# Retention phase: keys transposed by DMA, and the queries' product ahead of the state updates

## The chip, the cores and the metric

The kernel runs on one core of one Trainium2 chip. The metric is device time in microseconds (us); lower is better. The core's engines are TensorE (PE; its weight loads are listed as PEld), VectorE (DVE), ScalarE (ACT), GpSimd (POOL) and SyncE (SP, which here only issues DMA transfers). Each runs its own instructions in order and waits for others on semaphores.

## The reference

Two layers over 4 x 2048 tokens of 256 features. Each layer adds `s * silu(g)` to its input, where `s` is an attention and `g` a feed-forward network on the layer-normalised input. The change touches only the attention of the second layer, a retention:

```python
x = x + s * g
xn = _layernorm(x, axis=-1)
s = _L1_attn_ref(xn, L1_attn_W_q, L1_attn_W_k, L1_attn_W_v, L1_attn_W_o, L1_attn_gn_weight, L1_attn_gn_bias)
...
# inside _L1_attn_ref, 16 heads of 16 features
gammas = 1.0 - 2.0 ** (-5.0 - jnp.arange(h, dtype=jnp.float32))
q = (x @ W_q.T).reshape(b, t, h, dh)
k = (x @ W_k.T).reshape(b, t, h, dh)
v = (x @ W_v.T).reshape(b, t, h, dh)
decay = jnp.where(diff >= 0, gammas[:, None, None] ** pow_, 0.0)
attn = jnp.einsum('bihd,bjhd->bhij', q, k) * decay[None] / scale
y = jnp.einsum('bhij,bjhd->bihd', attn, v)
```

`y` is then normalised over tokens and heads and multiplied by `W_o`.

## The kernel before

The program is a row of phases, each with a block of instructions per engine and a barrier behind it. The phase in question is `phase_retention` (L1993 on). It goes over the 64 tiles of 128 tokens in a chunked form: a tile is cut into two sub-blocks of 64 tokens, the scores are computed within a sub-block, and what lies before it comes through a state (16 x 16 for each head) that is carried along.

Numbers are kept to more than f16 precision by splitting an operand into a high and a low f16 half and adding three products (high-high, low-high, high-low). ScalarE makes the high half (a copy to f16), GpSimd the low half (the f32 value minus the high half).

For a tile the stages are, by the names in the code:

- `project` (TensorE, six 128x512 matmuls through L213): keys and values into one PSUM bank of the tile's slot; `queries` (L2154, 12 matmuls): the queries into bank 2.
- `keys` (VectorE, L2232) scales the keys into `kd`, `keys_hi` (ScalarE, L2193) and `keys_lo` (GpSimd, L2285) split them into `kd16`. `values` on ScalarE (L2177) and VectorE (L2238) splits the values into `vpad`. `queries` on VectorE (L2246) scales the queries into `qd`, `queries_hi` (L2198) and `queries_lo` (L2291) split them.
- `turn` (TensorE, L2085): four 128x128 transposes of `kd16` into `turned`, the second half of PSUM bank 7. `keys_T` (ScalarE, L2185) spreads `turned` into `kx16` in two instructions.
- `spread` (SyncE, L2049): four transfers that lay the values out as `v16`.
- `scores` (TensorE, L2070, 48 small matmuls) into the first halves of banks 0 to 3; `masked` (VectorE, L2225) multiplies them with the causal mask into `pm`; `scores_hi` (ScalarE, L2203) and `scores_lo` (GpSimd, L2297, two halves of 128x512) split them.
- `updates` (TensorE, L2101, 48 small matmuls): the state's additions, into the second halves of banks 0 and 1. `states` (VectorE): L2252 adds them to the state, L2257 applies the decay (both inputs in SBUF), L2259 adds the second sub-block. `next_state` (L2267, both tensor inputs in SBUF) makes the state for the next tile. `states_hi` (L2210) and `states_lo` (L2303) split it.
- `results` (TensorE, L2121 and L2130, 48 matmuls each) into the first half of bank 7; `keep_result` (ScalarE, L2166) saves them; `statistics` (VectorE, L2274) reads them.

The order of each engine's work is written by hand as a list of (skew, stage) for `pipeline`: in step c the stage runs for tile c - skew. The first and last steps are unrolled, the rest is a hardware loop of three steps, since buffers have three slots (`U = 3`). On TensorE:

```python
pipeline(pe, TILES, [(4, scores), (3, turn), (0, project), (3, updates), (2, queries), (5, results)], 3, head=0)
```

On VectorE: masked, keys, values, states, queries, next_state, statistics. On ScalarE: keep_result, states_hi, keys_hi, values, keys_T, queries_hi, scores_hi. On GpSimd: states_lo, keys_lo, queries_lo, scores_lo. On SyncE only spread.

Waits that the change and the prediction use (`ago(t, n)` means: the work of the tile n before t): `scores` waits for `s_t1` of its own tile (L2259, because the updates share its PSUM banks) and for the queries' scaling (`s_qd`) of the next tile. `updates` waits for the masking of the step's scores (`s_p`), and so does `queries`. `results` waits for the split scores and states, for `v16`, for `keep_result` of the tile before, and for `keys_T` (`s_kx`), because both use PSUM bank 7.

Of the kernel before, what the change touches and what calls it, by code (L numbers as in the profile page):

```python
# [28 lines left out]
P = 128  # L29
D = 256  # L30
# [1965 lines left out]
def phase_retention(nc, ps, xT_all, w1, tables, ident, ystat, yT_all, late):  # L1996
# [4 lines left out]
    with Phase(nc, "ret") as ph:  # L2001
# [6 lines left out]
        kx16 = late[:, scores_w:scores_w + keys_w].rearrange("p (u a c s e j) -> p u a c s e j", u=U, a=2, c=C, s=SUBS, e=2)  # L2008
        qd = ph.sb("qd", [P, U, C, P])
# [5 lines left out]
        (s_fill, s_zero, s_kv, s_q, s_vhi, s_vlo, s_kd, s_qd, s_kdhi, s_kdlo, s_qhi, s_qlo, s_turn, s_kx, s_u, s_t0, s_r1,  # L2015
         s_t1, s_r0, s_sthi, s_stlo, s_s, s_p, s_phi, s_plo, s_y, s_yev, s_stat, s_pass, s_spass) = ph.sems(
            "fill zero kv q vhi vlo kd qd kdhi kdlo qhi qlo turn kx u t0 r1 t1 r0 sthi stlo s p phi plo y yev stat pass spass")
        s_vx = [ph.sem(f"vx{n}") for n in range(U)]
# [5 lines left out]
        turned = ps[:, 7, D:2 * D].bitcast(F16)  # L2024
# [13 lines left out]
        @block.sync  # L2038
        def _(sp):
            def spread(t):  # L2040
                sp.wait_ge(s_y, ago(t, 3))
                through(sp, s_spass)
                sp.wait_ge(s_vlo, after(t))
                sp.wait_ge(s_vhi, after(t))
                for s in range(SUBS):
                    for e in range(2):
                        src = vpad[s * SUB:(s + 1) * SUB, t.slot4, e * 2 * D:(e + 1) * 2 * D]
                        dst = v16[e * SUB:(e + 1) * SUB, t.slot4, s].rearrange("p k d -> p (k d)")
                        sp.dma_start(dst, src).then_inc(s_vx[t.slot4], 16)  # L2049
            pipeline(sp, TILES, [(3, spread)], 3)  # L2050

        @block.tensor
        def _(pe):
            prime_wrap(pe, s_kv, s_q, s_turn, s_u, s_s, s_y)
# [22 lines left out]
            def turn(t):  # L2077
                pe.wait_ge(s_kdhi, after(t))
                pe.wait_ge(s_kdlo, after(t))
                pe.wait_ge(s_kx, ago(t, 1))  # L2080
                pe.wait_ge(s_yev, ago(t, 3))
                for part in range(2):
                    for c in range(C):
                        at = (part * C + c) * P
                        ins = pe.transpose(turned[:, at:at + P], kd16[:, t.slot4, part, c * P:(c + 1) * P], ident[:])  # L2085
                ins.then_inc(s_turn, 1)

            def updates(t):
# [17 lines left out]
            def results(t):  # L2106
# [6 lines left out]
                if not isinstance(t.n, int) or t.n + 2 < TILES:  # L2113
                    pe.wait_ge(s_kx, ago(t, -2))
# [42 lines left out]
            pipeline(pe, TILES, [(4, scores), (3, turn), (0, project), (3, updates), (2, queries), (5, results)], 3, head=0)  # L2157

        @block.scalar
        def _(act):  # L2160
# [19 lines left out]
            def keys_T(t):  # L2180
                act.wait_ge(s_turn, after(t))
                act.wait_ge(s_s, ago(t, 3))
                src = turned.rearrange("p (k j) -> p k j", j=SUB)
                for e in range(2):
                    ins = act.activation(kx16[:, t.slot4].rearrange("p a c s e j -> p (a c s) e j")[:, :, e], src,  # L2185
                                         ACT.Copy, scale=parity[:, e:e + 1])
                ins.then_inc(s_kx, 1)

            def keys_hi(t):
                act.wait_ge(s_kd, after(t))  # L2190
                act.wait_ge(s_u, ago(t, 3))
                act.wait_ge(s_turn, ago(t, 3))
                act.activation(kd16[:, t.slot4, 0], kd[:, t.slot4], ACT.Copy).then_inc(s_kdhi, 1)  # L2193
# [21 lines left out]
        def _(dve):  # L2215
# [60 lines left out]
            pipeline(dve, TILES, [(4, masked), (1, keys), (1, values), (3, states), (2, queries), (3, next_state),  # L2276
# [328 lines left out]
```

## Time and profile before

| | us |
|---|---|
| median of 3 runs (1788.99 to 1789.36) | 1789.06 |
| the profiled execution | 1786.93 |
| its span in the profile | 1785.0 |
| busy in the span: PE / DVE / ACT / POOL | 1376.5 / 1372.3 / 1255.4 / 1221.4 |

The span is the time from the first to the last instruction in the profile; the profiled execution's own time is 1.9 us more. Busy times are sums over phases with different limits, so the share of an engine over the whole span says little about one phase. The retention phase fills the span from about 1363.5 to 1714 us. All times in rows are microseconds from the span's start unless marked ns.

In a timeline row stand: start, length, engine, line, operation, output <- inputs, how many instructions were merged, and in brackets how long the engine had been idle before it and what let it go. "issue" there means that nothing in the profile shows what it waited for. Waiting and register instructions of an engine are not shown. Matmul ends are modelled.

### The profile page before, as it was taken

To read this page: it belongs to the slowest core of one execution; us is meant where nothing else is said; L and a number is where in the kernel's file an instruction comes from. 1 tells how busy PE (TensorE), PEld (TensorE's weight loads), DVE (VectorE), ACT (ScalarE), POOL (GpSimd) and SP (SyncE) were. 2 spreads that over 40 slices of the span, in tenths; PEclk is the share of its full clock that TensorE was granted. 3 is DMA by queue.
4 is the path that set the end of the run, shared out by engine and by line. 5 is a ranking of instruction groups with operands and counts; after the bars stand their busy time and mean duration, and the time that the engine had idled before them with its cause. 6 is when DMAs were issued, how large, how long until landed. Compare 5 with 4: busy or idle time off the path is not lost. (4 is left out here: it accounts for less than half of the span.)

```text
span 1785.0 us, 63408 instructions
## 1 busy us (share of the span) xinstructions
PE 1376.5 (77%) x21895; PEld 952.6 (53%) x21896; DVE 1372.3 (77%) x3576; ACT 1255.4 (70%) x3382; POOL 1221.4 (68%) x1312
## 2 busy tenths in 40 slices
PE   3549999969889745455544899999997799999857
PEld 2515555545555434344432566666664566666646
DVE  7876777766566479988856999999984688888748
ACT  7727888856566558778837888888754677777745
POOL 6738777743333488777615899999974677777747
PEclk9999999989999968778767999999998999999969
DMA  7626777779999657665644566665653122222238
GB/s 258 224 95 180 190 194 194 192 161 202 207 216 222 174 168 187 186 176 156 181 104 97 114 123 129 127 129 119 120 106 70 44 53 53 51 50 52 54 95 290
DMA packets 495360, 256.33 MB, mean 144 GB/s; under 512 B 359357, under 2 KB 484864, under 8 KB 494720
## 3 DMA queue, kind: packets, MB, share of 16 engines
q1 hardware_dynamic: 482658, 219.11, 51.0%
q0 software_dynamic: 12576, 35.67, 6.5%
q8 instruction: 64, 1.05, 0.3%
q14 instruction: 62, 0.51, 0.1%
HBM read 79.52 MB, written 73.44 MB: 86 GB/s over the span
## 5 line engine op out<-in xcount | busy, mean ns | idle before, releaser
L213 PE MATMUL ps<-all_late,l_xq_T 128*128 128x352 f16 x1536 | 252.6, 316 | 57.1 <-DMA l_xq_T<-l_apart 30.5
L213 PEld LDWEIGHTS ps<-all_late,l_xq_T 128*128 (+1 forms) x1536 | 146.9, 99 | 149.2 <-DVE ffn_h L711 45.8
L213 PE MATMUL ps<-l0moe_W,all_xT_all 128*128 128x16 f16 (+2 forms) x1152 | 191.2, 313 | 38.4 <-ACT all_xT_all L912 22.3
L1444 POOL TENSOR_TENSOR all_late<-experts_se,all_mhalf 128x4 f32<-128x4 f32 (+1 forms) x77 | 76.5, 993 | 160.1 <-DVE experts_se L1553 154.1
L2297 POOL TENSOR_TENSOR all_late<-ret_pm,all_late 128x512 f16<-128x512 f32 x128 | 145.7, 1160 | 19.3 <-ACT all_late L2203 19.3
L213 PEld LDWEIGHTS ps<-l0moe_W,all_xT_all 128*128 128x128 f16 x1152 | 84.2, 100 | 120.8 <-ACT all_xT_all L912 26.0
L619 PE MATMUL ps<-all_late,ffn_hT 128*128 128x256 f16 x1088 | 131.7, 276 | 9.4 <-ACT l_xq_T L683 6.0
L1709 PE MATMUL ps<-l_kvm,both_q 128*128 128x136 f16 x384 | 39.6, 275 | 120.3 <-DVE both_o L1882 108.2
L213 PE MATMUL ps<-moe_E,experts_gT 128*128 x864 | 117.5, 276 | 15.8 <-DMA experts_gT<-slots_dram 11.1
L619 PEld LDWEIGHTS ps<-all_late,ffn_hT 128*128 128x128 f16 x1088 | 106.7, 99 | 29.8 <-issue 7.1
L2225 DVE TENSOR_TENSOR ret_pm<-ps,l_apart 128x1024 f32<-128x1024 f32 x64 | 78.4, 1225 | 41.1 <-PE ps L2070 40.1
L364 POOL TENSOR_TENSOR ffn_h<-ffn_fq_val,ffn_h 128x704 f16<-128x704 f32 x64 | 97.6, 1525 | 14.8 <-ACT ffn_h L359 14.7
L1709 PEld LDWEIGHTS ps<-l_kvm,both_q 128*128 128x128 f16 x384 | 33.8, 123 | 126.4 <-issue 126.1
L213 PE MATMUL ps<-l_W,all_xT_all 128*128 128x512 f16 x384 | 95.5, 386 | 3.8 <-DVEq L1993 2.9
L213 PEld LDWEIGHTS ps<-moe_E,experts_gT 128*128 128x128 f16 x864 | 71.1, 98 | 50.9 <-issue 31.7
L417 POOL TENSOR_TENSOR ffn_fq_val<-ffn_fq_big,ffn_fq_step 128x704 f32<-128x704 bf16 x64 | 89.5, 1398 | 12.5 <-POOL ffn_h L364 8.6
L2185 ACT ACTIVATE all_late<-ps,l_apart 128x512 f16<-128x512 f16 x128 | 81.5, 695 | 18.5 <-PE ps L2085 18.5
L1517 ACT ACTIVATE all_late<-ps 128x510 f32<-128x510 f32 x72 | 42.9, 596 | 72.3 <-PE ps L1493 51.3
L2166 ACT ACTIVATE all_xT_all<-ps 128x256 f32 (+1 forms) x64 | 24.6, 384 | 89.1 <-PE ps L2130 89.1
L2291 POOL TENSOR_TENSOR ret_q<-ret_qd,ret_q 128x256 f16<-128x256 f32 x64 | 43.0, 672 | 63.4 <-ACT ret_q L2198 63.4
L1744 POOL DMA_INDIRECT both_y<-rows_dram,moe_pos_lo x64 | 73.6, 1150 | 18.1 <-issue 17.0
L213 PE MATMUL ps<-moe_E,experts_hT 128*128 x432 | 69.2, 274 | 19.8 <-DMA experts_hT<-experts_hs 7.0
(299 smaller groups left out, 4705.3 us busy)
## 6 DMA issues: line engine op xcount, KB each, us to landing
rows_dram<-all_late SPq DMA_DIRECT2D x72, 256.0 KB
ret_v<-ret_vpad SPq DMA_DIRECT2D x256, 64.0 KB
front_xin<-x SPq DMA_DIRECT2D x16, 512.0 KB, 4.2
x_dram<-front_x SPq DMA_DIRECT2D x16, 512.0 KB, 5.0
all_late<-x_dram SPq DMA_DIRECT2D x64, 128.0 KB
z_dram<-all_late SPq DMA_DIRECT2D x64, 128.0 KB
both_zin<-z_dram SPq DMA_DIRECT2D x16, 512.0 KB
both_xin<-x SPq DMA_DIRECT2D x16, 512.0 KB
```

The costliest lines, as they stand in the source:

```text
L213: mm = pe.matmul(out, lhs[a], rhs[b], start=first and n == 0, stop=last and n == 2, skip_group_check=True)
L364: eng.tensor_tensor(lo, self.shaped(t, hi), hi, ALU.subtract).then_inc(self.lo, 1)
L417: pool.tensor_tensor(self.b3(self.val[:, u]), self.b3(self.big[:, u]), self.wide(self.step[:, u, 0:self.blocks]), ALU.mult).then_inc(self. ...
L619: ins = pe.matmul(down_ps, hT[:, t.slot, c % both], DN[:, c], start=c == 0, stop=c == both + FFC - 1, skip_group_check=True)
L1444: pool.tensor_tensor(rows[:, n % 4, which, :, 0], se[:, u, which], power[:, which], ALU.pow).then_inc(s_time, 1)
L1517: act.activation(os[t.slot4][:, :, 1:D], op[t.slot], ACT.Copy, scale=1 / WS).then_inc(s_oc, 1)
L1709: ins = pe.matmul(nps[:, k, c], q16[:, t.slot, a, c, k * P:(k + 1) * P], kv[b], start=c == 0 and n == 0, stop=n == 2, skip_group_check=True)
L1744: pool.indirect_dma_start(dst[:, slot, k], None, rows_dram, at).then_inc(arrived[slot], 16)
L2185: ins = act.activation(kx16[:, t.slot4].rearrange("p a c s e j -> p (a c s) e j")[:, :, e], src, ACT.Copy, scale=parity[:, e:e + 1])
L2225: dve.tensor_tensor(pm[:, t.slot4], sps, causal[:].unsqueeze(1).to_broadcast([P, 4, RC]), ALU.mult).then_inc(s_p, 1)
L2291: pool.tensor_tensor(q16[:, u, 1], qd[:, u], q16[:, u, 0], ALU.subtract).then_inc(s_qlo, 1)
L2297: ins = pool.tensor_tensor(p16[:, u, 1, r], pm[:, u, r], p16[:, u, 0, r], ALU.subtract)
```

## The change

1. `turn` moves from TensorE to SyncE. Its four transposes become one transposing DMA transfer from `kd16` into new SBUF buffers `kT` (three slots, one of them in spare room of `late`), issued in the step of tile c - 2, behind the step's `spread`. `keys_T` on ScalarE, still at skew 3, reads `kT` instead of PSUM.
2. `turned` in PSUM bank 7 is gone, and with it the wait of `results` for `keys_T`. `updates` takes over the waits for both halves of `kd16`. `keys_hi` waits for the landing of the transfer that read its slot before.
3. On TensorE `queries` (tile c - 2) now stands in front of `updates` (tile c - 3); on VectorE the scaling of the queries stands in front of `states`.

```diff
+        kT = [ph.sb(f"kT{n}", [P, 2 * C, P], F16)[:] for n in range(U - 1)]
+        kT.append(late[:, scores_w + keys_w:scores_w + keys_w + 2 * C * P].rearrange("p (k m) -> p k m", m=P))
...
-        turned = ps[:, 7, D:2 * D].bitcast(F16)
...
-            pipeline(sp, TILES, [(3, spread)], 3)
+
+            def turn(t):
+                sp.wait_ge(s_kx, ago(t, 3))
+                through(sp, s_spass)
+                sp.wait_ge(s_kdhi, after(t))
+                through(sp, s_spass)
+                sp.wait_ge(s_kdlo, after(t))
+                through(sp, s_spass)
+                sp.dma_start_transpose(kT[t.slot4], kd16[:, t.slot4].rearrange("p k d -> p (k d)")
+                                       ).then_inc(s_turn[t.slot4], 16)
+            pipeline(sp, TILES, [(3, spread), (2, turn)], 3)
...
-            def turn(t):
+            def updates(t):
                 pe.wait_ge(s_kdhi, after(t))
                 pe.wait_ge(s_kdlo, after(t))
-                pe.wait_ge(s_kx, ago(t, 1))
-                pe.wait_ge(s_yev, ago(t, 3))
-                for part in range(2):
-                    for c in range(C):
-                        at = (part * C + c) * P
-                        ins = pe.transpose(turned[:, at:at + P], kd16[:, t.slot4, part, c * P:(c + 1) * P], ident[:])
-                ins.then_inc(s_turn, 1)
-
-            def updates(t):
                 pe.wait_ge(s_vhi, after(t))
...
                 pe.wait_ge(s_yev, ago(t, 1))
-                if not isinstance(t.n, int) or t.n + 2 < TILES:
-                    pe.wait_ge(s_kx, ago(t, -2))
...
             def keys_T(t):
-                act.wait_ge(s_turn, after(t))
+                act.wait_ge(s_turn[t.slot4], 16 * (t.n // U) + 16)
                 act.wait_ge(s_s, ago(t, 3))
-                src = turned.rearrange("p (k j) -> p k j", j=SUB)
+                src = kT[t.slot4].rearrange("p k (s j) -> p (k s) j", j=SUB)
...
                 act.wait_ge(s_u, ago(t, 3))
-                act.wait_ge(s_turn, ago(t, 3))
+                if not isinstance(t.n, int) or t.n >= U:
+                    act.wait_ge(s_turn[t.slot4], 16 * (t.n // U))
```

TensorE, one full step of the unrolled part (tile c - 4's scores to tile c - 5's results), before (-) and after (+); the loop repeats this order:

```order
-L2070 MATMUL ps<-ret_q,all_late 128x64 x48
-L2085 MATMUL ps<-all_ident,ret_kd 128x128 x4
+L2081 MATMUL ps<-ret_q,all_late 128x64 x48
 L213 MATMUL ps<-l_W,all_xT_all 128x512 x6
-L2101 MATMUL ps<-ret_vpad,ret_kd 32x32 x48
 L2154 MATMUL ps<-all_xT_all,l_W 128x128 x12
+L2103 MATMUL ps<-ret_vpad,ret_kd 32x32 x48
 L2121 MATMUL ps<-all_late,ret_v 32x64 x48
 L2130 MATMUL ps<-ret_q,ret_st 32x64 x48
```

L2085, the four transposes, is gone, and the 48 updates matmuls (L2101, now L2103) have moved from in front of the 12 queries matmuls to between them and results.

VectorE, the same step, before:

```order
L2225 TENSOR_TENSOR ret_pm<-ps,l_apart 128x1024
L2232 TENSOR_TENSOR ret_kd<-ps,l_apart 128x256
L2238 SCALAR_TENSOR_TENSOR ret_vpad<-ps,ret_vpad 128x8x16 x2
L2252 SCALAR_TENSOR_TENSOR ret_told<-ps,ret_state 128x64
L2257 TENSOR_TENSOR ret_state<-ret_told,l_apart 128x64
L2259 SCALAR_TENSOR_TENSOR ret_told<-ps,ret_state 128x64
L2246 TENSOR_TENSOR ret_qd<-ps,l_apart 128x256
L2267 SCALAR_TENSOR_TENSOR ret_state<-ret_told,l_apart 128x64
```

and after:

```order
L2226 TENSOR_TENSOR ret_pm<-ps,l_apart 128x1024
L2233 TENSOR_TENSOR ret_kd<-ps,l_apart 128x256
L2239 SCALAR_TENSOR_TENSOR ret_vpad<-ps,ret_vpad 128x8x16 x2
L2247 TENSOR_TENSOR ret_qd<-ps,l_apart 128x256
L2253 SCALAR_TENSOR_TENSOR ret_told<-ps,ret_state 128x64
L2258 TENSOR_TENSOR ret_state<-ret_told,l_apart 128x64
L2260 SCALAR_TENSOR_TENSOR ret_told<-ps,ret_state 128x64
L2268 SCALAR_TENSOR_TENSOR ret_state<-ret_told,l_apart 128x64
```

The scaling of the queries (L2246, now L2247) has moved from behind the three state operations to in front of them.

SyncE, the beginning of the hardware loop after the change (before, only the groups of four copies stood there):

```order
L142 ISA
L2044 REGISTER_ALU
L2050 DMA ret_v<-ret_vpad 64x512 x4
L2053 REGISTER_ALU
L2055 REGISTER_ALU
L2059 DMA_TRANSPOSE all_late<-ret_kd 128x4x128
```

One transposing transfer has been added behind the four copies of each step.

## Rows read from the trace of the kernel before

**Rows 1.** Busy time by stage: stretch, us, then PE, PEld, DVE, ACT, POOL, clock, DMA

```profile
1417.94:1687.06 269.12, 244.30 (x11346) 175.35 (x11345) 218.25 (x583) 194.56 (x480) 210.26 (x266) 1.00 0.22 52
```

**Rows 2.** Timeline of VectorE: masking, first and last of the steady state

```profile
1417.94 1.23 DVE L2225 TENSOR_TENSOR ret_pm<-ps,l_apart 128x1024 f32<-128x1024 f32 x1 [0.32 <-PE ps L2070]
...
1687.06 1.23 DVE L2225 TENSOR_TENSOR ret_pm<-ps,l_apart 128x1024 f32<-128x1024 f32 x1 [0.39 <-PE ps L2070]
```

**Rows 3.** Timeline of TensorE: parts of the loop's first step, the whole second

```profile
1503.80 0.55 PE L2070 MATMUL ps<-ret_q,all_late 32*128 32x64 f16 x48 [0.96 <-issue]
...
1506.01 0.52 PE L2101 MATMUL ps<-ret_vpad,ret_kd 64*32 64x32 f16 x48
...
1508.68 0.55 PE L2070 MATMUL ps<-ret_q,all_late 32*128 32x64 f16 x48 [0.23 <-issue]
...
1509.22 0.38 PE L2085 MATMUL ps<-all_ident,ret_kd 128*128 128x128 f16 x4
...
1509.46 1.47 PE L213 MATMUL ps<-l_W,all_xT_all 128*128 128x512 f16 x6
...
1510.86 0.52 PE L2101 MATMUL ps<-ret_vpad,ret_kd 64*32 64x32 f16 x48
...
1511.40 0.94 PE L2154 MATMUL ps<-all_xT_all,l_W 128*128 x12
...
1512.28 0.56 PE L2121 MATMUL ps<-all_late,ret_v 128*32 128x64 f16 x48
...
1512.76 0.55 PE L2130 MATMUL ps<-ret_q,ret_st 32*32 32x64 f16 x48
...
1513.51 0.55 PE L2070 MATMUL ps<-ret_q,all_late 32*128 32x64 f16 x48 [0.20 <-issue]
```

**Rows 4.** Timeline of the other engines, same two steps

```profile
1504.58 1.22 DVE L2225 TENSOR_TENSOR ret_pm<-ps,l_apart 128x1024 f32<-128x1024 f32 x1 [1.01 <-PE ps L2070]
...
1509.30 1.22 DVE L2225 TENSOR_TENSOR ret_pm<-ps,l_apart 128x1024 f32<-128x1024 f32 x1 [0.31 <-PE ps L2070]
...
1509.73 1.28 ACT L2185 ACTIVATE all_late<-ps,l_apart 128x512 f16<-128x512 f16 x2
...
1511.18 1.08 ACT L2203 ACTIVATE all_late<-ret_pm 128x1024 f16<-128x1024 f32 x1
...
1511.65 0.23 DVE L2252 SCALAR_TENSOR_TENSOR ret_told<-ps,ret_state 128x64 f32<-128x64 f32 x1 [0.40 <-PE ps L2101]
1511.91 0.24 DVE L2257 TENSOR_TENSOR ret_state<-ret_told,l_apart 128x64 f32<-128x64 f32 x1
1512.18 0.22 DVE L2259 SCALAR_TENSOR_TENSOR ret_told<-ps,ret_state 128x64 f32<-128x64 f32 x1
...
1512.34 2.28 POOL L2297 TENSOR_TENSOR all_late<-ret_pm,all_late 128x512 f16<-128x512 f32 x2 [0.27 <-ACT all_late L2203]
1512.38 0.42 DVE L2246 TENSOR_TENSOR ret_qd<-ps,l_apart 128x256 f32<-128x256 f32 x1
1512.73 0.85 DVE L2267 SCALAR_TENSOR_TENSOR ret_state<-ret_told,l_apart 128x64 f32<-128x64 f32 x1
```

**Rows 5.** Timeline of GpSimd and VectorE, one step of the loop's first turns

```profile
1408.62 2.27 POOL L2297 TENSOR_TENSOR all_late<-ret_pm,all_late 128x512 f16<-128x512 f32 x2 [0.27 <-ACT all_late L2203]
1408.86 1.00 DVE L2257 TENSOR_TENSOR ret_state<-ret_told,l_apart 128x64 f32<-128x64 f32 x1
```

**Rows 6.** Timeline of TensorE in the unrolled tail: updates, results behind it

```profile
1701.09 0.55 PE L2101 MATMUL ps<-ret_vpad,ret_kd 64*32 64x32 f16 x48 [1.03 <-issue]
1701.76 0.83 PE L2121 MATMUL ps<-all_late,ret_v 128*32 128x64 f16 x48
```

**Rows 7.** Timeline of SyncE: the last of the four copies of the second step

```profile
1510.50 0.60 SPq L2049 DMA_DIRECT2D ret_v<-ret_vpad  x1
```

**Rows 8.** Timeline of SyncE and TensorE in the experts phase: a transpose and who waited

```profile
450.74 1.22 SPq L1416 DMA_TRANSPOSE experts_hT<-experts_hs  x1
453.06 0.50 PE L213 MATMUL ps<-moe_E,experts_hT 128*128 x3 [1.89 <-DMA experts_hT<-experts_hs]
```

More of the change, by code:

```diff
@@ L2014, in phase_retention @@
         st16 = ph.sb("st16", [P, U, 2, SUBS, CW], F16)
-        (s_fill, s_zero, s_kv, s_q, s_vhi, s_vlo, s_kd, s_qd, s_kdhi, s_kdlo, s_qhi, s_qlo, s_turn, s_kx, s_u, s_t0, s_r1,
+        (s_fill, s_zero, s_kv, s_q, s_vhi, s_vlo, s_kd, s_qd, s_kdhi, s_kdlo, s_qhi, s_qlo, s_kx, s_u, s_t0, s_r1,
          s_t1, s_r0, s_sthi, s_stlo, s_s, s_p, s_phi, s_plo, s_y, s_yev, s_stat, s_pass, s_spass) = ph.sems(
-            "fill zero kv q vhi vlo kd qd kdhi kdlo qhi qlo turn kx u t0 r1 t1 r0 sthi stlo s p phi plo y yev stat pass spass")
-        s_vx = [ph.sem(f"vx{n}") for n in range(U)]
+            "fill zero kv q vhi vlo kd qd kdhi kdlo qhi qlo kx u t0 r1 t1 r0 sthi stlo s p phi plo y yev stat pass spass")
+        s_vx, s_turn = ([ph.sem(f"{n}{u}") for u in range(U)] for n in ("vx", "turn"))
         sps = ps[:, 0:4, 0:RC]
@@ L2049, in spread @@
                         sp.dma_start(dst, src).then_inc(s_vx[t.slot4], 16)
-            pipeline(sp, TILES, [(3, spread)], 3)
+            def turn(t):
[8 more added lines that the diff above has]
+            pipeline(sp, TILES, [(3, spread), (2, turn)], 3)
         @block.tensor
         def _(pe):
-            prime_wrap(pe, s_kv, s_q, s_turn, s_u, s_s, s_y)
+            prime_wrap(pe, s_kv, s_q, s_u, s_s, s_y)
             def scores(t):
@@ L2156, in queries @@
                 ins.then_inc(s_q, 1)
-            pipeline(pe, TILES, [(4, scores), (3, turn), (0, project), (3, updates), (2, queries), (5, results)], 3, head=0)
+            pipeline(pe, TILES, [(4, scores), (0, project), (2, queries), (3, updates), (5, results)], 3, head=0)
         @block.scalar
@@ L2275, in statistics @@
                 ins.then_inc(s_stat, 1)
-            pipeline(dve, TILES, [(4, masked), (1, keys), (1, values), (3, states), (2, queries), (3, next_state),
+            pipeline(dve, TILES, [(4, masked), (1, keys), (1, values), (2, queries), (3, states), (3, next_state),
                                   (7, statistics)], 3)
```

## The prediction

> **What bounds the kernel now.** I read the table by stages first. In the 269.12 us in which the retention phase is in steady state, TensorE is busy 244 us at a granted clock of 1.00, VectorE 218, GpSimd 210, ScalarE 195 and the DMA engines 22% [rows 1]. Nothing outside the retention phase is touched. Then the VectorE timeline for the length of a step. The masking product (L2225) comes once per step, and between its start at 1417.94 and its start at 1687.06 lie 53 steps [rows 2], so a step takes 5.08 us and three of them, one turn of the hardware loop, 15.23. Then TensorE through one step [rows 3]: scores at 1508.68, turn +0.54, project +0.24, updates +1.40, queries +0.54, results +0.88, second half of results +0.48, and the next scores +0.75, together 4.83. It waits only ahead of scores: about 0.2, and 0.96 where the loop closes [rows 3]. So TensorE's own order sets the step. Beside it, in the same step [rows 4]: VectorE starts masking 0.62 after scores (0.78 in the loop's first step) and needs 1.22; the three state operations take 0.75 from 1511.65; GpSimd begins the low half of the scores at 1512.34, 3.66 after scores.
>
> **TensorE's own part of the change.** Turn goes: 0.24 from its start to project's. Scores to project then costs 0.54 to 0.57; I take 0.56. Project used to be followed by updates after 1.40, now by queries. Both wait for the masking product of this step. In the loop's first step that product ended at 1505.81 and updates began at 1506.01 [rows 3, 4], so what waits for it starts 0.20 behind its end: 0.62 + 1.22 + 0.20 = 2.04 in an ordinary step, where project alone would let go at 1.96. So 0.08 of the 0.24 is lost at once. In the first step it is 0.78 + 1.22 + 0.20 = 2.20 before and after, and the removal of turn gives nothing.
>
> Next, queries to updates. Updates' waits now stand behind the long queries matmuls, as the waits of results did, so I take the old distance of queries to results, 0.88. Then updates to results. The four wait instructions of results now stand behind 48 short matmuls that the queue runs through quickly. Two rows bound this. With nothing to wait for, 48 such matmuls are followed after 0.48 to 0.54; behind the second half of results, where four waits for scores stand, the next starts 0.75 later, so the waits cost 0.27 [rows 3]. In the tail of the phase, results does follow updates directly: 1701.09 to 1701.76, 0.67 with one wait instruction fewer [rows 6]. So the distance lies between 0.54 (waits hidden) and 0.81; I take 0.81. Results to scores stays at 1.23, and 1.99 where the loop closes.
>
> Sum of TensorE alone: 2.04 + 0.88 + 0.81 + 1.23 = 4.96 in the second step, 2.20 + 0.88 + 0.81 + 1.23 = 5.12 in the first, 4.96 + 0.76 = 5.72 in the third, so 15.80 for three, against 15.23. The removed transposes are paid for by a wait that they used to cover and by waits that the queries used to cover: 0.19 a step slower, before anything else.
>
> **VectorE's part.** The states now follow the queries' scaling. In an ordinary step: queries on TensorE from 2.04, 0.94 long, their scaling on VectorE from 3.04 to 3.46 (it takes 0.42 [rows 3, 4]). Updates start at 2.92; their first state operation comes 0.6 to 0.8 later (1510.86 to 1511.65 is 0.79 [rows 3, 4]), so at 3.55 to 3.7. The second operation, L2257, whose two inputs both lie in SBUF, comes 0.26 later at 3.83. It used to come at 3.23. This is the crux, because GpSimd's scores work runs from 3.66 for 2.3 us. What happens to L2257 under it is in the trace: at 1408.86 it met a GpSimd operation that had begun at 1408.62 (two halves in 2.27), and took 1.00 instead of 0.24, ending 0.1 behind the first half [rows 5]. L2267, the state for the next tile, has the same kind of inputs and lies there too: 0.85 from 1512.73, ending 0.1 behind the first of the two halves that GpSimd had started at 1512.34 [rows 4]. L2252 and L2259 have one input in PSUM and seem not to be held: L2259 ended at 1512.40 in its usual 0.22, with GpSimd already at work [rows 4]. The Trainium skill says the same as a rule (SBUF — State Buffer, "SBUF: two separate sides"): the port pair shared by VectorE and GpSimd is an exclusive lock for a whole instruction, also against a VectorE operation with two SBUF inputs. The trace agrees with the 1.00 us just named; without such a lock the step would be the 4.96 above.
>
> The next scores wait for the last state operation (L2259), because both use the same PSUM banks; that wait had slack (L2259 ended at 1512.40, scores began at 1513.51) and now has none. I step through one turn of the loop, times from each step's scores; a scores group starts no earlier than 0.5 after the start of L2259 (its 0.22, and waits as above).
> First step: masking 0.78, queries 2.20, updates 3.08, results 3.89. ScalarE and GpSimd had run ahead during the loop's closing, so GpSimd starts its halves at 3.20, and L2257, which starts at 4.16, is let go behind the first one at 4.45. L2259 at 4.49; scores by TensorE at 5.11. Length 5.11.
> Second step: L2267 was held to the end of the second half, statistics and masking follow it, masking at 0.79 again; results 3.88; GpSimd from 3.69, L2257 starts at 4.00 and ends at 4.93, L2259 from 4.97; next scores at 5.47. Length 5.47.
> Third step: masking at 0.91, results at 3.99; GpSimd from 3.35, L2257 ends at 4.60; the loop closes, 3.99 + 1.99. Length 5.98.
> Sum 16.56. The same arithmetic gives 15.33 for the kernel before where the rows have 15.23, so I count 1.23 more per three steps, 0.41 each, over 53 steps: 21.7 us.
>
> **SyncE, DMA and ScalarE.** Every step gets a fifth transfer, the transpose of 128x512 f16. SyncE ends the issue of its four copies at 1511.10, 2.42 after scores [rows 7], by when GpSimd's low half of the keys is long there, and issues the transpose then. A transpose of the same shape in the experts phase took 1.22 to issue and was waited for until 2.32 behind the start of its issue [rows 8]. It lands some 2.6 + 2.3 = 4.9 in, and ScalarE wants it in the next step, at 4.96 + 1.05 = 6.0 (1509.73 is 1.05 behind scores [rows 4]). So it is hidden, with 1 us of slack; if it takes over 3.4 it is the bound. SyncE is free again at 3.9, before the next results end. Its cost is between 0 and, at twice the row's time, 0.9 a step; I take 0, since the row is of the same shape. The Trainium skill speaks against the move (VectorE: DVE Perf Modes, "The three transpose paths"): 390 ns for a 128x128 tile on TensorE against 1309 ns by DMA, and TensorE preferred where PSUM will do. By an estimate from that page four tiles one after the other would take 5.2 us, land at 7.8 and hold up every step by some 1.8; the row of the same shape, 2.32 for all four, says no.
> ScalarE's two spreading copies now read SBUF. The pair took 1.28 [rows 4]; its copy of 1024 elements from SBUF took 1.08 [rows 4], so one of 512 costs 0.54 at least, and hardly over the 0.7 that one of the pair takes now: no change to 0.1 less each. They no longer wait for turn, which starts GpSimd's scores work sooner, never later.
> Outside the 53 steps lie 11 that fill and empty the pipeline. The first tile's keys come some 2 us later (2.32 against turn's 0.4), once; the rest I leave. Term: +1.5.
>
> **Sum.** The profiled execution took 1786.93 us; 21.7 + 1.5 on it is 1810. The median of the runs is 1789.06, 2.1 above it; with the same +23.2 it is 1812.
>
> **Rivals.**
> First, L2257 slips past the lock. It starts at 3.83 to 4.0 against GpSimd's 3.66: if ScalarE's copies from SBUF are slower by 0.1 each, GpSimd starts after it. Then TensorE's 15.80 hold: 0.19 x 53 = 10, plus 1.5, 1801.
> Second, on the other side: TensorE is the bound and loses work. If the waits of results stay hidden (0.54) and the states are not held, the three steps are 15.80 - 0.81 = 14.99, 0.08 less a step, 4 us, and the 1.5 on top: 1786. If masking ran early enough too, all of turn's 0.24 would be gained in 64 steps: 1774. For it: TensorE is busy 91% [rows 1]. Against it: rows 5 and 6. It decides from the distance updates to results: under about 0.62 the kernel is faster if the lock does not hit.
> Third, the transposing transfer is late. At 4.5 us from issue to landing instead of 2.3 each step would be some 0.1 longer than forecast: 1818; beyond that 0.3 per 0.3, up to 1830.
> Fourth, gains and losses cancel within 0.2%: the waits hidden, the lock hitting one step of three.
>
> **How the numbers follow.** Chances: the forecast 0.52 (1805 to 1819), lock missed 0.22 (1796 to 1805), faster 0.12, late transfer 0.08, cancelled 0.06. A measurement tells about 0.2%, 3.6 us, from no change. Slower is 0.52 + 0.22 + 0.08 = 0.82, faster 0.12, same 0.06. The two cases of faster and same fall below 1794 and make up 0.18; 1794 to 1824 holds the rest but for the late transfer's far end.
>
> **What would show it.** In the profile after, the masking product should come every 5.5 us, in a pattern of 5.1, 5.5 and 6.0; L2257's median should rise from 0.23 to some 0.5 or more, and rows of it should end 0.1 behind GpSimd's L2297; the start of results should lie 0.8 behind updates, with idle of about 0.2 in front; no wait for the keys' transfer should show on ScalarE. Steps of 5.27 with L2257 still at 0.23 are the first rival; steps under 5.05 are the second; ScalarE waiting on a DMA ahead of L2185 is the third.

## The result and the profile after

| | kernel before | changed kernel |
|---|---|---|
| median, us | 1789.03 (4 runs) | 1820.05 (4 runs, 1815.98 to 1829.01) |
| the profiled execution, us | 1786.93 | 1821.12 |
| its span, us | 1785.0 | 1819.3 |

The ratio is 1.018, 95% interval 1.015 to 1.021: slower, and clear of the noise, at the far end of the range of 1794 to 1824, with 1812 forecast.

Busy time by stage of the changed kernel. Columns: stretch, us, then PE, PEld, DVE, ACT, POOL, granted clock, DMA share. The first row answers to [rows 1]:

```profile
1422.05:1719.88 297.83, 237.00 (x11130) 164.93 (x11129) 241.07 (x584) 199.89 (x479) 211.55 (x267) 0.99 0.31 70
1422.05:1534.00 111.95, 90.59 (x4218) 62.94 (x4217) 89.99 (x224) 76.80 (x185) 81.20 (x103) 1.00 0.32 73
1538.00:1542.00 4.00, 3.91 (x66) 2.23 (x64) 2.13 (x5) 2.06 (x4) 2.52 (x3) 0.62 0.34 75
```

The first masking of this stretch starts at 1422.05 and the last at 1719.88, and 53 steps lie between, as in [rows 2]: 297.83 us against 269.12. That is 28.7 us more, 0.54 a step. VectorE is busy 23 us longer with the same work, and TensorE 7 us shorter. GpSimd's time has hardly changed (211.6 against 210.3). VectorE does the same operations, so some of them must read longer than before; the rows below show which.

The other 5.6 us of the 34.3 that the span grew: from the first masking (1375.34, before 1374.18) to the start of the stretch 46.71 against 43.76, from its end to the last masking (1740.23 and 1706.13) 20.35 against 19.07. Of the remaining 1.4, 1.2 had come about ahead of the first masking. In the spans of all kernels below that start lies anywhere from 1370.9 to 1376.1, so I don't count it as the change's.

TensorE in the third step of a loop turn (the loop's first step follows the closing gap). It answers to [rows 3]:

```profile
1508.83 0.55 PE L2081 MATMUL ps<-ret_q,all_late 32*128 32x64 f16 x48 [0.57 <-DVE ret_told L2260]
1509.39 1.47 PE L213 MATMUL ps<-l_W,all_xT_all 128*128 128x512 f16 x6
1511.10 0.89 PE L2154 MATMUL ps<-all_xT_all,l_W 128*128 x12 [0.25 <-DVE ret_pm L2226]
1511.92 0.52 PE L2103 MATMUL ps<-ret_vpad,ret_kd 64*32 64x32 f16 x48
1512.72 0.55 PE L2121 MATMUL ps<-all_late,ret_v 128*32 128x64 f16 x48 [0.27 <-issue]
```

GpSimd and VectorE ahead of it, at the end of the second step. They answer to [rows 4]:

```profile
1506.99 2.27 POOL L2298 TENSOR_TENSOR all_late<-ret_pm,all_late 128x512 f16<-128x512 f32 x2 [0.27 <-ACT all_late L2204]
1507.13 0.23 DVE L2253 SCALAR_TENSOR_TENSOR ret_told<-ps,ret_state 128x64 f32<-128x64 f32 x1 [0.18 <-PE ps L2103]
...
1507.38 0.85 DVE L2258 TENSOR_TENSOR ret_state<-ret_told,l_apart 128x64 f32<-128x64 f32 x1
...
1508.27 0.22 DVE L2260 SCALAR_TENSOR_TENSOR ret_told<-ps,ret_state 128x64 f32<-128x64 f32 x1
```

Read downwards, this is the forecast mechanism. GpSimd starts its first half at 1506.99. The decay of the state (L2258, both inputs in SBUF) starts at 1507.38 and is done at 1508.23, 0.1 behind that half. L2260 follows, and the scores at 1508.83 come 0.56 behind its start. TensorE sat idle for 0.57 before them. On its own path, queries started 2.27 behind scores (the masking from 1509.66 to 1510.86 in between), updates 0.82 behind queries, results 0.80 behind updates with 0.27 idle.

The waits by releaser, window 1420 to 1740 (us in total, times, longest):

```profile
DVE ret_qd L2247 <- PE ps L2154: 33.0, 55, 1.8
PE ps L2081 <- DVE ret_told L2260: 28.3, 33, 1.2
...
PE ps L2121 <- issue: 14.4, 53, 0.3
PE ps L2154 <- DVE ret_pm L2226: 12.1, 34, 1.6
```

Neither of the two TensorE waits for VectorE stands in the waits of before. The longest scores wait, 1.2, is not explained by a hold until the end of a first half. It shows up first here, in GpSimd, VectorE and TensorE together:

```profile
1534.15 2.27 POOL L2298 TENSOR_TENSOR all_late<-ret_pm,all_late 128x512 f16<-128x512 f32 x2 [0.27 <-ACT all_late L2204]
...
1534.81 0.23 DVE L2253 SCALAR_TENSOR_TENSOR ret_told<-ps,ret_state 128x64 f32<-128x64 f32 x1
...
1535.35 1.15 DVE L2258 TENSOR_TENSOR ret_state<-ret_told,l_apart 128x64 f32<-128x64 f32 x1 [0.31 <-DVE ret_told L2253]
...
1537.11 0.55 PE L2081 MATMUL ps<-ret_q,all_late 32*128 32x64 f16 x48 [1.23 <-DVE ret_told L2260]
1537.69 2.74 PE L213 MATMUL ps<-l_W,all_xT_all 128*128 128x512 f16 x6
```

The two halves of L2298 take 2.27 together, 1.16 each by their median. This is the loop's first step. L2258 asks at 1535.35, 1.20 behind the first half's start, so it has just missed the change from one half to the other and is held until the second ends at 1536.42. One loop turn earlier it came 1.03 behind and took 0.23:

```profile
1517.74 2.28 POOL L2298 TENSOR_TENSOR all_late<-ret_pm,all_late 128x512 f16<-128x512 f32 x2 [0.27 <-ACT all_late L2204]
...
1518.77 0.23 DVE L2258 TENSOR_TENSOR ret_state<-ret_told,l_apart 128x64 f32<-128x64 f32 x1 [0.31 <-DVE ret_told L2253]
```

Less than 0.2 us decides between 0.23 and 1.15. The miss left TensorE idle for 1.23, and behind that its granted clock fell: it was 0.62 in the 4 us of the third row of the first view above, 0.50, the lower of its two levels (1.2 GHz), in the 3 us of the first row here, and 1.00 again afterwards:

```profile
1538.00:1541.00 3.00, 3.00 (x14) 1.53 (x13) 1.71 (x4) 2.06 (x4) 1.52 (x2) 0.50 0.45 100
1544.00:1620.00 76.00, 60.00 (x2780) 41.64 (x2780) 62.65 (x147) 52.38 (x124) 53.68 (x69) 1.00 0.31 71
```

The six project matmuls took 2.74 instead of 1.47. The idle time alone doesn't explain the fall: in the 53 steps TensorE sat idle for 1.13 to 1.23 ahead of scores eleven times, and the clock fell behind two of them. From there on one step in three meets the second half. Until 1534 three steps took 16.4 to 16.6 us, afterwards 16.9, and 18.0 and 17.9 where the clock fell (there is a second fall at 1623 to 1626). Sorting the 53 rows of L2258 by when they start against GpSimd: 34 were held to the end of the first half (17.5 us over their usual 0.23 in sum), 12 into the second (9.8 us), 7 not. In the kernel before none of the 53 was. There it is the operation for the next state (L2267) that is held, with a median of 0.85 over its 64 rows, where the same operation takes 0.28 in g4 below.

### The profile page after: what moved, and what is told of

The parts are those of the page before. It is cut to its first block and busy times, and to the rows that moved or that the text cites. A ratio compares the mean times of both kernels' runs of the same rounds, so it can differ in the third digit from the quotient of the medians.

```text
span 1819.3 us, 63214 instructions
## 1 busy us (share of the span) xinstructions
PE 1371.0 (75%) x21639; PEld 942.9 (52%) x21640; DVE 1395.9 (77%) x3576; ACT 1261.7 (69%) x3382; POOL 1221.3 (67%) x1312
## 3 DMA queue, kind: packets, MB, share of 16 engines
q8 instruction: 63, 1.03, 0.3%
## 5 line engine op out<-in xcount | busy, mean ns | idle before, releaser
L2298 POOL TENSOR_TENSOR all_late<-ret_pm,all_late 128x512 f16<-128x512 f32 x128 | 145.5, 1158 | 25.1 <-ACT all_late L2204 25.1
L213 PE MATMUL ps<-l_W,all_xT_all 128*128 128x512 f16 x384 | 101.6, 405 | 4.7 <-DVEq L1993 2.7
L2226 DVE TENSOR_TENSOR ret_pm<-ps,l_apart 128x1024 f32<-128x1024 f32 x64 | 77.8, 1216 | 16.3 <-PE ps L2081 15.9
L1744 POOL DMA_INDIRECT both_y<-rows_dram,moe_pos_lo x64 | 74.0, 1156 | 18.1 <-issue 17.3
L404 ACT ACTIVATE ffn_fq_big<-ps 128x704 bf16<-128x704 f32 x64 | 48.4, 756 | 51.2 <-DVE ps L397 51.1
```

The costliest lines, as they stand in the source:

```text
L213: mm = pe.matmul(out, lhs[a], rhs[b], start=first and n == 0, stop=last and n == 2, skip_group_check=True)
L404: act.activation(self.big[:, u], self.work[u], ACT.Abs, scale=self.MAGIC).then_inc(self.mg, 1)
L1744: pool.indirect_dma_start(dst[:, slot, k], None, rows_dram, at).then_inc(arrived[slot], 16)
L2226: dve.tensor_tensor(pm[:, t.slot4], sps, causal[:].unsqueeze(1).to_broadcast([P, 4, RC]), ALU.mult).then_inc(s_p, 1)
L2298: ins = pool.tensor_tensor(p16[:, u, 1, r], pm[:, u, r], p16[:, u, 0, r], ALU.subtract)
```

## The experiments

Each kernel was timed beside the kernel before. "53 steps" is the same stretch as above, from the profiled execution (before: 269.1 us, changed kernel: 297.8), and "3 steps" the usual length of one loop turn in it (15.26; 16.4, then 16.9).

| kernel | median, us | ratio to before (95%) | 53 steps | 3 steps |
|---|---|---|---|---|
| f1, transfer, old orders | 1799.96 | 1.0067 (1.0048 to 1.0086) | 277.1 | 15.7 |
| f2, new orders, turn on TensorE | 1813.28 | 1.0137 (1.0118 to 1.0157) | 290.3 | 16.4 |
| f3, changed kernel, the decay not held | 1802.80 | 1.0085 (1.0064 to 1.0106) | 280.0 | 15.8 |
| f4, f1 with scores' waits early | 1800.99 | 1.0072 (1.0052 to 1.0092) | 279.4 | 15.5 to 16.0 |
| g1, f1, the decay not held | 1795.17 | 1.0052 (1.0031 to 1.0073) | 273.6 | 15.3 to 15.6 |
| g2, g1 with the masking's wait last | 1786.75 | 1.0001 (0.9989 to 1.0013) | 265.9 | 15.0 |
| g3, f3 with results' waits early | 1803.10 | 1.0096 (1.0075 to 1.0117) | 280.0 | 15.9 |
| g4, changed kernel, GpSimd in quarters | 1805.14 | 1.0112 (1.0091 to 1.0134) | 282.4 | 16.0 |
| h1, before with the masking's wait last | 1785.69 | 0.9990 (0.9978 to 1.0001) | 267.8 | 15.15 |
| h2, g2 with turn left on TensorE | 1786.79 | 1.0000 (0.9990 to 1.0010) | 267.6 | 15.14 |

The medians are of 4 to 12 runs and the last two columns of one execution; f1's profiled execution (1794.94) was its fastest, 5.0 below the median. So a difference of a us or two between two kernels in the 53 steps says little.

### f2: the orders alone

```diff
-[(4, scores), (3, turn), (0, project), (3, updates), (2, queries), (5, results)]
+[(4, scores), (3, turn), (0, project), (2, queries), (3, updates), (5, results)]
-[(4, masked), (1, keys), (1, values), (3, states), (2, queries), (3, next_state),
+[(4, masked), (1, keys), (1, values), (2, queries), (3, states), (3, next_state),
```

> The transposes stay on TensorE as before; only queries stands in front of updates on TensorE and the queries' scaling in front of the states on VectorE. Theory (the order costs): at least the changed kernel's loss, since turn's 0.24 a step comes on top where masking does not hide it: TensorE alone 5.12 + 5.12 + 5.88 = 16.1 for three steps, with the held L2257 16.6 to 17.2: 1813 to 1826 us, and the median of L2257 well above 0.5 us. Rival (the transfer costs): within 5 us of the kernel before, 1784 to 1794.

Measured: 1813.28, and 21.2 us more in the 53 steps. Every one of the 53 decays was held to the end of a first half, 25.2 us in sum. GpSimd and VectorE of one step:

```profile
1608.65 2.27 POOL L2297 TENSOR_TENSOR all_late<-ret_pm,all_late 128x512 f16<-128x512 f32 x2 [0.27 <-ACT all_late L2203]
...
1609.12 0.77 DVE L2257 TENSOR_TENSOR ret_state<-ret_told,l_apart 128x64 f32<-128x64 f32 x1
```

So the orders do most of the damage, without any transfer. No decay met a second half here, and the rhythm stayed at 16.4. Which of the two orders, TensorE's or VectorE's, does it was not tested.

### f3: the decay's hold taken away

`told` of the first sub-block goes to a free part of PSUM bank 3, so L2258 has one input in PSUM.

```diff
+        told0 = [ps[:, 3, RC + u * CW:RC + (u + 1) * CW] for u in range(U)]
...
-                dve.scalar_tensor_tensor(told[:, u, 0], ups[:, 0], ...
+                dve.scalar_tensor_tensor(told0[u], ups[:, 0], ...
...
-                dve.tensor_tensor(state[:, v, 1], told[:, u, 0], sdecay[:], ALU.mult)...
+                dve.tensor_tensor(state[:, v, 1], told0[u], sdecay[:], ALU.mult)...
```

> The changed kernel, but the first sub-block's sum (told of sub-block 0) is written to free columns of PSUM bank 3 instead of SBUF, so that L2257's operation has only one input in SBUF. Theory (GpSimd's work holds that operation): its median falls back from 0.78 to 0.23 us, scores no longer wait for it, TensorE's 15.8 for three steps remain: 1800 to 1803 us, against 1820. Rival (late updates alone set the step, the hold is slack): 1815 or more, with the operation short but the step the same.

Measured: 17 us under the changed kernel. The decay's 64 rows in one line (min/median/max ns), first of the changed kernel:

```profile
L2258 DVE TENSOR_TENSOR ret_state<-ret_told,l_apart x64: 224/777/1212, 1373.0 to 1736.5; 128x64 f32<-128x64 f32 x64
```

and of f3:

```profile
L2259 DVE TENSOR_TENSOR ret_state<-ps,l_apart x64: 224/224/226, 1371.6 to 1716.9; 128x64 f32<-128x64 f32 x64
```

The decay is no longer held, and what remains is mostly TensorE's own path: 15.84 per three steps, where its sum in the prediction was 15.80. The other operation with two SBUF inputs, the one for the next state, still is held, though less; the changed kernel, then f3:

```profile
L2268 DVE SCALAR_TENSOR_TENSOR ret_state<-ret_told,l_apart x64: 284/695/1131, 1373.6 to 1737.2; 128x64 f32<-128x64 f32 x64
L2269 DVE SCALAR_TENSOR_TENSOR ret_state<-ret_told,l_apart x64: 285/532/1220, 1372.1 to 1717.4; 128x64 f32<-128x64 f32 x64
```

### g4: the hold shortened

```diff
-for r in (slice(0, 2), slice(2, 4)):
+for r in (slice(0, 1), slice(1, 2), slice(2, 3), slice(3, 4)):
```

> The changed kernel, but GpSimd makes the low half of the scores in four operations of 128x256 instead of two of 128x512, 0.67 us each by the rows of that shape, 0.4 us more in all. Theory (the state operation is held to the end of the GpSimd operation that it meets): its maximum falls from 1.21 to about 0.75, its median from 0.78 to 0.4 to 0.6, and the kernel is 5 to 15 us faster than the changed one, 1805 to 1815. Rival (it is slowed by sharing, in proportion to the overlap, or held to the end of all of GpSimd's scores work): its time stays or grows, and the kernel's with it, 1820 or more.

Measured: 15 us under the changed kernel (13 by the two ratios to the kernel before, 15.4 in the 53 steps). The decay's line:

```profile
L2258 DVE TENSOR_TENSOR ret_state<-ret_told,l_apart x64: 224/378/728, 1369.7 to 1719.6; 128x64 f32<-128x64 f32 x64
```

The longest decay went from 1.21 to 0.73, with the length of the GpSimd operation (0.67 a quarter). That is the second proof, by another route, that it is GpSimd's operation that holds L2258. Not all of the 15 us is the decay's: the operation for the next state came free as well, and with it the masking behind it.

```profile
L2268 DVE SCALAR_TENSOR_TENSOR ret_state<-ret_told,l_apart x64: 283/285/336, 1370.2 to 1720.2; 128x64 f32<-128x64 f32 x64
```

The four quarters cost GpSimd 2.61 instead of 2.27 a step, and it can afford them.

### f1: the transfer alone

The changed kernel with both orders as before (on TensorE scores, project, updates, queries, results).

> Only the turning of the keys goes to the transposing transfer; TensorE and VectorE keep the order of the kernel before (updates before queries, states before the queries' scaling). Theory (the order costs, the transfer is hidden): an ordinary step has updates at 2.04 (masking), queries +0.54, results +0.88, scores +1.23, so 4.69 instead of 4.83; the loop's first 4.85, its third 5.45; three together 14.99 against 15.23, which is 4 us less over 53 steps, and 1.5 more at the start: about 1786 us. The operation L2257 keeps a median of 0.23 us. Rival (the transfer is what costs, by its issue on SyncE or its landing): near the changed kernel, about 1815 to 1820 us, with ScalarE waiting for a DMA in front of keys_T.

Measured: 1799.96, slower than before by 0.67% where I expected equal or better. This was the surprise of the study. The loop's first step, three engines:

```profile
1600.81 1.23 DVE L2226 TENSOR_TENSOR ret_pm<-ps,l_apart 128x1024 f32<-128x1024 f32 x1 [0.75 <-POOL all_late L2298]
...
1602.39 0.52 PE L2103 MATMUL ps<-ret_vpad,ret_kd 64*32 64x32 f16 x48 [0.37 <-DVE ret_pm L2226]
...
1603.35 2.27 POOL L2298 TENSOR_TENSOR all_late<-ret_pm,all_late 128x512 f16<-128x512 f32 x2 [0.28 <-ACT all_late L2204]
1603.42 1.16 DVE L2258 TENSOR_TENSOR ret_state<-ret_told,l_apart 128x64 f32<-128x64 f32 x1 [0.19 <-DVE ret_told L2253]
...
1605.47 0.55 PE L2081 MATMUL ps<-ret_q,all_late 32*128 32x64 f16 x48 [0.63 <-DVE ret_qd L2247]
```

Two things differ from the kernel before. Updates starts 0.35 behind the end of the masking, where it was 0.20 [rows 3, 4]. And one decay in three, the one of the loop's first step, meets the first half of L2298, here by 0.07 us. One turn on, the decay asks 3.41 behind scores and GpSimd starts 3.34 behind them, where the kernel before has 3.24 and 3.56: updates is later, and GpSimd earlier. In the 53 steps nobody waits for the transfer itself.

### f4: is it the waits ahead of scores?

```diff
             def scores(t):
-                pe.wait_ge(s_kx, after(t))
-                pe.wait_ge(s_qhi, after(t))
-                pe.wait_ge(s_qlo, after(t))
...
             def results(t):
+                    pe.wait_ge(s_kx, ago(t, -2))
+                    pe.wait_ge(s_qhi, ago(t, -2))
+                    pe.wait_ge(s_qlo, ago(t, -2))
```

On f1; scores keeps these waits for the first two tiles.

> As the kernel with the transfer alone, and in addition three of the waits of scores (keys_T and both halves of the queries) are made one step earlier, ahead of the results, where long matmuls stand in front. Theory (the wait instructions themselves, not what they wait for, make the 0.2 us gap in front of scores): the gap falls by 0.1 to 0.2, 5 to 10 us less than the kernel with the transfer alone. Rival (scores really waits for the last state operation or the queries' scaling): the same time as with the transfer alone, within 2 us.

Measured: the same time as f1, but not because the waits are free. TensorE ahead of scores in the 53 steps, f1 and then f4:

```profile
PE ps L2081 <- issue: 15.4, 36, 0.8
PE ps L2082 <- issue: 7.8, 17, 0.6
```

With the waits for VectorE its idle time there fell from 25.7 to 13.8 us. In exchange 5.6 came up ahead of results, where the three waits now stand, updates' rose from 13.8 to 17.3, and the median of the decay from 0.31 to 0.69 in these steps. The waits were moved, and what they gained was lost elsewhere.

### g1 and g2: the two effects of f1, one after the other

g1 is f1 with `told` in PSUM as in f3. g2 adds one moved line in `updates`:

```diff
-                pe.wait_ge(s_p, ago(t, 1))
                 pe.wait_ge(s_t1, ago(t, 1))
+                pe.wait_ge(s_p, ago(t, 1))
                 through(pe, s_pass)
```

> The transfer alone (order of before), and the first sub-block's sum in PSUM, so that the second state operation has one input in SBUF. In the run with the transfer alone that operation took 1.16 us in one step of every three, the step of 5.29. Theory (the transfer costs because GpSimd's scores work now starts earlier in the loop's first step and holds that operation): the 5.29 falls to 4.85 to 4.95, three steps to 15.2 to 15.3, the time by 6 to 9 us to 1790 to 1794. Rival (SyncE or the transfer itself slows the step): no change, 1798 to 1801.

> As g1, and in updates the wait for the masking stands last of six instead of fifth, so that it is in the last of the three wait instructions instead of the first. In the run with the transfer alone updates began 0.33 to 0.38 behind the end of masking, where the kernel before took 0.20. Theory (the two wait instructions behind the one for the masking are the difference, 0.1 each): updates follow the masking by 0.17 to 0.2 again, 0.1 to 0.2 a step less, 5 to 10 us under g1. Rival (the instructions behind are free): the same time as g1.

Measured: g1 1795.17, 3.5 us less than f1 in the 53 steps and less than expected. That isn't what all holding is worth: the decay came free, but the operation for the next state is held longer, 48.3 us in the 53 steps where f1 has 32.0. g2 1786.75, another 7.7 us less in the 53 steps, which is the expected size. The next state, masking and updates of g1:

```profile
1602.32 1.27 DVE L2269 SCALAR_TENSOR_TENSOR ret_state<-ret_told,l_apart 128x64 f32<-128x64 f32 x1
...
1603.90 1.20 DVE L2227 TENSOR_TENSOR ret_pm<-ps,l_apart 128x1024 f32<-128x1024 f32 x1
...
1605.46 0.52 PE L2104 MATMUL ps<-ret_vpad,ret_kd 64*32 64x32 f16 x48 [0.51 <-DVE ret_pm L2227]
```

and of g2:

```profile
1602.19 1.22 DVE L2227 TENSOR_TENSOR ret_pm<-ps,l_apart 128x1024 f32<-128x1024 f32 x1 [0.61 <-PE ps L2082]
...
1603.67 0.52 PE L2104 MATMUL ps<-ret_vpad,ret_kd 64*32 64x32 f16 x48
```

From the end of the masking to updates it is 0.36 in g1 and 0.26 in g2. The masking ends last of all that updates waits for, and what stands behind its wait in the queue is then paid in the open. That is 0.10 a step, 5 us in 53 steps; the rest goes with the masking, which in g1 starts late in one step of these rows (0.96 behind the scores at 1602.94, behind the held operation) and not in g2 (0.62 behind those at 1601.57). This last part is read from the rows, not tested.

### h1 and h2: is that a gain of its own?

h1 moves the same line in the kernel before, h2 puts `told` in PSUM there as well.

> The kernel before, with one line moved: updates() waits for the masking (s_p) last instead of ahead of s_t1 and s_pass. Theory (the place of this wait matters only where the masking ends last ahead of updates, as it does once keys_T no longer waits for the turn on TensorE): in the kernel before, updates follows project without idle time in the steady part, so nothing changes: 1785 to 1790 us, ratio within 0.2%. Rival (the order of these waits is a gain of its own, whatever the turn does): 5 to 8 us less, as between g1 and g2: 1778 to 1783 us; then the transfer still costs these 5 to 8 us in g2.

> The kernel before with both edits of g2 and the turn left on TensorE: told of sub-block 0 in PSUM bank 3, and updates' wait for the masking last. It is g2 without the transfer. Theory: the scaling by decay had a median of 0.23 us here, so the lock costs next to nothing and neither does the order of the waits: 1783 to 1790 us, and g2 (1.0001 of the kernel before) shows that the transfer alone, with both repaired, costs or gains less than 0.3%. Rival: the two edits gain here too: 1776 to 1782 us, and the transfer alone costs 6 to 10 us even with both.

Measured: 0.9990 and 1.0000. In the kernel before the moved line is worth 1.4 us of 269, both edits 1.5, and nothing that shows in the time, since there updates waits for project and no decay is held. So g2 beside h2 is the price of the transfer with its two side effects repaired: 1786.75 and 1786.79. In the one profiled execution of each, the 53 steps are 1.7 us shorter (265.9 against 267.6) and the filling and emptying 1.6 us longer (66.0 against 64.4); the timed runs of either spread over 5 to 6 us, so neither is clear of the noise.

### g3: the waits of results hoisted

On f3, the six waits of `results` become a stage of their own ahead of `queries`.

> The changed kernel with the first sub-block's sum in PSUM (as f3), and the six waits of results moved ahead of the queries' product, where long matmuls are queued. Theory (the wait instructions of results, no longer covered by the queries, cost 0.25 a step): results follow updates by 0.54 instead of 0.8, about 13 us less than f3: 1788 to 1792 us. Rival (something else sets the distance): within 3 us of f3's 1803.

Measured: no gain, 1803.10 where 1788 to 1792 was expected. TensorE and VectorE of one step:

```profile
1599.79 1.15 DVE L2271 SCALAR_TENSOR_TENSOR ret_state<-ret_told,l_apart 128x64 f32<-128x64 f32 x1 [0.16 <-DVE ret_told L2263]
...
1601.25 1.20 DVE L2229 TENSOR_TENSOR ret_pm<-ps,l_apart 128x1024 f32<-128x1024 f32 x1
...
1602.69 0.90 PE L2157 MATMUL ps<-all_xT_all,l_W 128*128 x12 [0.67 <-DVE ret_pm L2229]
...
1603.52 0.52 PE L2104 MATMUL ps<-ret_vpad,ret_kd 64*32 64x32 f16 x48
...
1603.97 0.63 PE L2124 MATMUL ps<-all_late,ret_v 128*32 128x64 f16 x48
```

Updates to results did fall, from 0.80 to 0.45, so the waits are what filled that distance. The gain went into VectorE. Its operation for the next state (L2271 here, L2268 in the changed kernel) also has two SBUF inputs and was left as it was. It is held for 1.15 here, and statistics and masking queue behind it, without idle time. The masking starts 1.28 behind this step's scores (1599.97), and queries waits 0.67 for it. Over the 53 steps this wait grew from 9.0 us in f3 to 20.8, and VectorE's idle time for scores ahead of masking fell from 20.6 to 1.5. VectorE has become the bound, through the same hold on another operation. It wasn't tried to free that one too.

## Why the prediction came out as it did

**Turn removed, first wait exposed: right.** Forecast was scores to queries 2.04 for TensorE alone, and 2.33 in the third step of the walk through the turn (masking at 0.91, 1.22 long, 0.20 behind it). The row, which is of a third step, has 2.27: the masking starts 0.83 behind scores (the next state's operation ahead of it on VectorE is held too), and queries 0.24 behind its end. Queries to updates: 0.88 forecast, 0.82 measured.

**Updates to results: right.** 0.81 forecast at the upper of two bounds, 0.80 measured, 0.27 idle; g3 shows that it is the waits, and also that freeing them would have gained nothing, since VectorE is next. As a whole TensorE's own path was forecast at 15.80 per three steps and 10 us in 53; f3 has 15.84 and 10.9. That the sums meet is in part luck: f3's three steps are 5.20, 5.17 and 5.46 on average, where the sum had 5.12, 4.96 and 5.72. The masking comes late in the second step too (0.79), and results to scores where the loop closes takes 1.74, not 1.99.

**The hold: mechanism right, size too small.** Forecast was 11.7 of the 21.7 us. Taking the decay's hold away (f3 against the changed kernel) gives 17.8. Up to 1534 the sum was good, 16.4 to 16.6 for three steps where it had 16.56, but the steps weren't: from 1514.40 on they are 5.26, 5.60 and 5.60, forecast 5.11, 5.47 and 5.98. The third was let off by the closing of the loop, with 1.7 from results to scores instead of 1.99. The term that failed is the hold in the loop's first step. There L2257 was to ask at 4.16, 0.96 behind GpSimd's start at 3.20, and to be let go behind the first half. The rows have 4.38 and 3.34, 1.04 behind, in the turn from 1514.40, and 4.49 and 3.30 in the turn from 1530.86: past the end of the first half, held to the end of the second, and 6.25 long instead of 5.11. I wrote down one outcome where less than 0.2 us later there was another, 1.15 instead of 0.23. When it came, the loop turns grew from 16.4 to 16.9, nine times, and to 18.0 and 17.9 where the clock fell: 9 x 0.5 + 2 x 1.5 = 7.5, about the missing 28.7 - 21.7. It wasn't tested what would have happened without the first miss; that it set off the rest is read from the order of the rows. The other three timed runs of the changed kernel spread from 1815.98 to 1829.01, wider than any other kernel here, which fits a rhythm that can tip at different places.

**Filling: too small.** 1.5 forecast, 4.2 measured inside the phase (3.0 in front, 1.3 behind). I counted the late keys of the first tile alone. It isn't the decay's hold either: f3 has 3.3 and 1.4 in the same places, and f1 1.6 and 1.1. It wasn't taken apart further, but the granted clock is part of what differs. From the first masking to the 53 steps it was 0.85, where the kernel before had 0.96:

```profile
1375.34:1422.05 46.71, 34.93 (x1375) 23.41 (x1374) 29.31 (x72) 26.05 (x63) 27.34 (x36) 0.85 0.34 63
1374.18:1417.94 43.76, 32.68 (x1404) 22.45 (x1401) 28.44 (x71) 25.07 (x60) 26.62 (x33) 0.96 0.17 40
```

Behind the 53 steps it was 0.55 against 0.78. In f3 the two are 0.93 and 0.57, in f1 0.96 and 0.69. How much of the 4.2 us is the clock's stays open.

**The transfer: hidden as forecast, but not free.** ScalarE waited for it 3.3 us in all, at the first three tiles. The copies of `keys_T` take 722 ns, where they took 698 before: 0.02 more each, forecast no change to 0.1 less. What I had not priced is what moves along with it. `updates` took over two waits, its masking wait became the last to be fulfilled, and 0.35 instead of 0.20 lie between. I had put that 0.20 into the sum from a row of the kernel before, with its number of waits. In the changed kernel this hardly mattered, since queries waits for the masking there with few waits behind it (0.24 to 0.27). Alone, in f1, it cost more than the held decay: 7.7 us came back with it in g2, 3.5 with the decay in g1.

**The rivals.** "Lock missed" at 1801 is f3's 1802.8, so its price was right and its condition didn't hold. "Faster" needed updates to results under 0.62 and no hold. Neither came. "Late transfer" is out. "Cancelled" had the lock hit one step of three; it hit 46 of 53. The falls of the clock and the second half were in none of them, and neither was the placing of the masking's wait.

## What to carry to other kernels

Where two engines may shut each other out, compute the start of the one against each boundary of the other, and if it falls within 0.2 us of one, price both sides; putting one operand in PSUM, or cutting the other engine's operation smaller, is a cheap cure to try first (17 and 15 us here). Look at all such operations of the loop together: with the decay free, the next one of its kind was held longer in g1, and in g3 once TensorE ran ahead. When a stage is moved on TensorE, move its waits in thought as well: long matmuls ahead of a group cover them, 48 short ones don't, and the wait that is fulfilled last belongs at the end of the list. Taking 0.24 us a step off the busiest engine gained 1.7 us at most in 53 steps and nothing in the whole here, even with its side effects repaired, since a wait for VectorE stood right behind it.

## What the runs showed of the hardware

- A held VectorE operation counts as busy: L2258 reads 224 ns unhindered and up to 1212 under GpSimd. It is the length of the GpSimd operation that it meets that sets the hold, and between two operations in a row it gets in only if it asked before the second began: 0.23 when it came 1.03 or, at 1469.55, 1.11 behind the first one's start, 1.15 when it came 1.20 behind. The Trainium skill (SBUF — State Buffer, "SBUF: two separate sides") calls the shared port an exclusive lock for a whole instruction, and these rows agree; with one input in PSUM all 64 rows lie between 224 and 226 ns.
- TensorE's granted clock fell from 1.00 to 0.50 (1.2 GHz), for a mean of 0.62 over 4 us, in the middle of steady work. TensorE had been busy 81% of the time up to 1534 (90.59 of 111.95) and sat idle for 1.23 right before. Nine more idle times of 1.13 us and over were not followed by a fall, so what sets it off stays open. In the kernel before, at 91%, the clock was 1.00 throughout [rows 1].
- Waits on TensorE that no matmuls cover cost time: moving one line of waiting from behind to ahead of the one fulfilled last took the distance from 0.36 to 0.26 (g1, g2), and hoisting the six of results took 0.80 to 0.45 (g3).
- A DMA transpose of 128x512 f16 took 1.19 us to issue on SyncE (median of 43). ScalarE could use the second tile's 2.45 us behind the start of the issue, close to the 2.32 of [rows 8]:

```profile
1373.60 1.20 SPq L2059 DMA_TRANSPOSE ret_kT<-ret_kd  x1
1376.05 1.33 ACT L2185 ACTIVATE all_late<-ret_kT,l_apart 128x512 f16<-128x512 f16 x2 [0.69 <-DMA ret_kT<-ret_kd]
```
